# A recurrence step reordered: query times key, its masking and the next right sides

## The reference

```
attn  = where(causal, q_i @ k_i.T, 0)
u_adj = u_i - w_i @ S                      # u = T vc, w = T kbc, T the inverse of a triangular matrix
o_i   = q_i @ S + attn @ u_adj
S     = S + k_i.T @ u_adj
```

## Time and profile before

| | us |
|---|---|
| median of 3 runs (2459.3 to 2461.65) | 2460.59 |
| profiled execution, its own time | 2465.9 |
| its span | 2463.3 |
| TensorE busy | 2157.7 (88%) |
| VectorE busy | 1235.2 (50%) |
| ScalarE busy | 905.7 (37%) |
| GpSimd busy | 576.3 (23%) |

### The profile page before, as it was taken

One profiled execution on the slowest core, in us unless ns is written; L12 is line 12 of the kernel. 1 busy time (PEld: TensorE's weight loads), 2 busy tenths in 40 slices (PEclk: granted clock), 3 DMA queues, 4 the chain that ended last, 5 costly groups with the idle time before them and its releaser, 6 DMA issues.

```text
span 2463.3 us, 40437 instructions
## 1 busy us (share of the span) xinstructions
PE 2157.7 (88%) x15412; PEld 1857.6 (75%) x15412; DVE 1235.2 (50%) x1846; ACT 905.7 (37%) x1420; POOL 576.3 (23%) x416
## 2 busy tenths in 40 slices
PE   7887865655799999944999999999999999999998
PEld 5776755555688888833888888888888888888887
DVE  5776757896556776755143323432343233323332
ACT  4454530002233333324344434443444344434442
POOL 2555555896343444310000000000000000000000
PEclk9999977887799999976999999999999999999999
DMA  3558768787877887733000000000000000000000
GB/s 128 189 197 204 198 194 202 195 210 243 223 179 177 197 206 191 170 119 124 1 18 17 0 17 17 17 0 17 17 17 0 17 17 17 0 17 17 18 1 18
DMA packets 342570, 234.45 MB, mean 95 GB/s; under 512 B 280946, under 2 KB 315250, under 8 KB 331890
## 3 DMA queue, kind: packets, MB, share of 16 engines
q1 hardware_dynamic: 334258, 232.65, 34.2%
q10 hardware_dynamic: 8256, 1.05, 0.4%
HBM read 145.31 MB, written 88.34 MB: 95 GB/s over the span
## 4 chain that ended last, share of the span: by engine, by line
PE 51%; issue 1%; DVE 1%; ACT 0%; DMA 0%; POOL 0%; DVEq 0%; SPq 0%; ACTq 0%; POOLq 0%
PE B L1611 46%; PE O L1639 5%; PE T L1569 1%; DVE yb L1738 0%; ACT gate L1677 0%; DMA x<-x_s 0%; DVE stats L1769 0%; ACT L1677 0%; DVE z L1764 0%; DVE xl L1718 0%; DVE z L1760 0%; DVE z L1783 0%; ACT xh L1665 0%; POOL rstd L1819 0%; DVEq L1733 0%
## 5 line engine op out<-in xcount | busy, mean ns | idle before, releaser
L1611 PE MATMUL B<-act1l,wr 128*128 128x512 f32 x1024 | 398.5, 389 | 0.0
L1611 PE MATMUL B<-act0h,wr 128*128 128x512 f32 x1024 | 398.3, 389 | 0.0
L1611 PE MATMUL B<-act0l,wr 128*128 128x512 f32 x1024 | 398.3, 389 | 0.0
L1611 PE MATMUL B<-act1h,wr 128*128 128x512 f32 x1024 | 398.3, 389 | 0.0
L1691 ACT ACTIVATE yb<-B,scol 128x512 f32<-128x512 f32 x256 | 176.2, 688 | 581.1 <-PE B L1611 581.1
L1726 DVE TENSOR_TENSOR act0l<-yb,act0h 128x512 fp32r<-128x512 f32 x256 | 176.1, 688 | 378.0 <-ACT act0h L1694 375.8
L1816 POOL TENSOR_TENSOR rstd<-mv,ln_eps 128x4 f32<-128x4 f32 x16 | 3.2, 199 | 1305.0 <-DVE mv L1777 1305.0
L378 DVE SCALAR_TENSOR_TENSOR acc<-proj,taps,acc 128x512 f32<-128x512 f32 x288 | 214.4, 750 | 95.2 <-ACT acc L333 86.6
L1726 DVE TENSOR_TENSOR act1l<-yb,act1h 128x512 fp32r<-128x512 f32 x128 | 88.6, 692 | 295.5 <-ACT act1h L1694 295.5
L223 PE MATMUL proj<-xt,w_qkv 128*128 128x262 f32 x768 | 195.7, 402 | 37.7 <-DMA xt<-in_xt 20.9
L1611 PEld LDWEIGHTS B<-act1h,wr 128*128 128x128 f32 x1024 | 192.3, 188 | 39.9
(11 more groups left out here) (163 smaller groups left out, 3468.6 us busy)
## 6 DMA issues: line engine op xcount, KB each, us to landing
qk_s<-yT SPq DMA_DIRECT2D x16, 1024.0 KB, 5.8
kk_s<-kfull SPq DMA_DIRECT2D x16, 1024.0 KB, 3.9
qk<-qk_s SPq DMA_DIRECT2D x16, 1024.0 KB, 5.4
lt<-kk_s SPq DMA_DIRECT2D x15, 1024.0 KB, 5.3
wraw<-in_ffn_w SPq DMA_DIRECT2D x11, 1024.0 KB, 7.3
toe<-in_firp SPq DMA_DIRECT2D x64, 160.0 KB, 3.3
xt<-in_xt SPq DMA_DIRECT2D x16, 524.0 KB, 3.9
k_s<-ktok SPq DMA_DIRECT2D x16, 512.0 KB, 3.8
```

The source lines that it names most:

```text
L1611: last = nc.tensor.matmul(B[slot % 4][:, :], w, part, start=(k == 0 and i == 0), stop=(k == kts - 1 and i == len(parts) - 1))
```

## The change

In the ring's list, Q moves from behind W to behind T (for a step with both: N, T, Q, W, A, B, C). TensorE issues Q right behind T, ahead of the waits of the solve. VectorE evacuates Q as the first thing of its step, and computes the right side of step t+1 behind C's eviction of step t, ahead of the head norm and the layer norm; the right side of step 0 stands ahead of the first step. The streams of ScalarE, GpSimd and SyncE are as they were. No instruction is added or left out.

```diff
--- before.py
+++ after.py
@@ -843,7 +843,7 @@
         def rounds(pre, tail):
             n, q, a, b, c = ([(kind, g, "act" if kind in "NAB" else "dve") for g in range(4)] for kind in "NQABC")
             t, w = ([(kind, g, "act" if kind == "T" else "dve") for g in range(2)] for kind in "TW")
-            return (n if pre else []) + (t if tail else []) + (w if tail else []) + (q + a + b + c if pre else [])
+            return (n if pre else []) + (t if tail else []) + (q if pre else []) + (w if tail else []) + (a + b + c if pre else [])
 
         PRE, FULL, LAST = rounds(True, False), rounds(True, True), rounds(False, True)
 
@@ -1084,13 +1084,14 @@
                     from_state(t, p)
                     run("N", *rest)
                     run("T", *rest)
+                    run("Q", *rest)
 
                     pe.wait_ge(edges_done, t + 1)
                     pe.wait_ge(dve_out, last_c)
                     solve(t, p)
                     run("W", *rest)
                     outputs(t, p, n)
-                    run("QABC", *rest)
+                    run("ABC", *rest)
 
                 run("NQABC", PRE, 0, 0, 0, 0, 0, 0)
                 d, a = used(PRE, "dve"), used(PRE, "act")
@@ -1291,12 +1292,11 @@
                     last.then_inc(x1_done, 1)
 
                 def step(t, p, ntail, seq, round0, dve0, act0, pre, tail):
-                    right_side(t, p)
+                    if pre:
+                        evacuate("Q", seq, round0, t + 1, 1 - p)
                     if tail:
                         residual(t - 1, 1 - p, ntail, seq, round0)
                     outputs(t, p)
-                    if pre:
-                        evacuate("Q", seq, round0, t + 1, 1 - p)
                     head_sums(t)
                     if tail:
                         spread(t - 1, 1 - p, dve0 + used(seq, "dve", 1 + next(i for i, x in enumerate(seq) if x[:2] == ("W", 1))))
@@ -1308,6 +1308,7 @@
                         add_term("B", seq, act0, t + 1, 1 - p)
                     if pre:
                         evacuate("C", seq, round0, t + 1, 1 - p)
+                        right_side(t + 1, 1 - p)
                     head_norm(t)
                     if tail:
                         layer_norm(t - 1, 1 - p)
@@ -1331,6 +1332,7 @@
                         dve.wait_ge(act_out, 4)
                         dve.wait_ge(second_in, 16)
                         nc.vector.tensor_copy(lt[:, :, :], att[1][:, :, :]).then_inc(lt_moved, 1)
+                right_side(0, 0)
                 step(0, 0, 0, PRE, NPRE, used(PRE, "dve"), used(PRE, "act"), True, False)
                 with dve.Fori(0, MID // 2) as i:
                     for j in range(2):
```

## The result

The changed kernel takes 2469.43 us (median of 11 runs, 2464.47 to 2472.51) against 2460.59 before (11 runs, 2457.89 to 2462.53): a ratio of 1.0035, 95% interval 1.0027 to 1.0044, 6.6 to 10.8 us more. It is slower, as forecast, and inside the range; the forecast of 1.0024 lies just under the interval. The profiled execution of the changed kernel took 2466.87 us (span 2464.7), only 1.0 above that of before, so the profiles are compared stage by stage and not by their spans: the first N of the recurrence starts at 623.96 us after and at 627.09 before, and the feed-forward part behind the stage is 2.0 us shorter after, in code that the change does not touch.

What follows compares the result with a forecast made beforehand. TensorE was taken to bound the recurrence, with one 1.50 us hole per step. Fourteen intervals +4.8, step 0 +2.0 and the last step -1.0 made +5.8 us: 2466.4 us, ratio 1.0024, range 2460 to 2474.

Steps and rivals of the forecast that it cites:

- Step 1: On TensorE, query times key moved behind T costs its full 2.00 us per step, with no new waits.
- Step 2: Behind the state update, A starts at once; ScalarE's squares, ending at 3.87, delay its copies; TensorE alone starts N at 9.64.
- the rival in which the C eviction does not hold N: N starts at 9.64, 0.41 earlier than forecast; +0.1 us in all, 2460.7, no change; chance 0.28.
- Step 3: VectorE between mixture sum and C eviction gains 1.30 us, not 2.48; N waits for that eviction, starts at 10.05.
- Step 4: Right sides go ahead of head norm and layer norm, ready long before the solve; saves 0.24 us per step, 3.3 in all.
- the second stall: In some steps a long layer norm delays the right sides and the solve waits; forecast to go, 3.3 us in all.
- The sum: Whole kernel: period 27.30 us, fourteen intervals +4.8, first step +2.0, last step -1.0, together +5.8 us.
- the rival of the late loads: N waits for a last diagonal block landing 1.5 us later; +14 us on top, about 2480; chance 0.08.
- step 15: Last step of the recurrence, without query times key; solve forecast to start at 14.0 instead of 14.99, -1.0 us.
- step 0: First step of the recurrence, ahead of its first state update; query times key there forecast to add +2.0 us.

Runs made afterwards that it cites:

- experiment 3: Changed kernel with VectorE's layer-norm statistics put ahead of the head sums: 2458.06 us, ratio 0.9998 to the kernel before.
- experiment 4: Changed kernel with ScalarE's squares put behind the four A copies: 2485.14 us, ratio 1.0101 to the kernel before.
- experiment 9: Kernel before with one edit, VectorE's masks ahead of the sum with the mixture: 2511.39 us, ratio 1.0195.
- Experiment 2: Kernel before with one edit, the next step's right sides behind C, ahead of the head norm: 2459.63 us, ratio 0.9996.
- experiment 5: Changed kernel with squares behind A copies, statistics and add A ahead of head sums: 2459.0 us; second kernel, statistics also ahead of outputs: 2457.64 us.
- experiment 6: Second kernel of experiment 5 with key products and diagonal blocks loaded some 7 us earlier: 2473.66 us, ratio 1.0053 to the kernel before.
- experiment 8: Kernel before, query times key unmoved, masks ahead of the mixture sum, other reorderings: 2444.47 us with blocks loaded early, 2441.0 us with loads as before.

## Why the prediction was right

By its own steps:

- *Step 1, query times key counts in full:* right. It takes 2.0 us between T and the solve in every step, its data, its banks and W wait for nothing.
- *Step 2, ScalarE's squares are late next:* right. They end at 3.87, B waits 1.43 (about 1.3 named), products from the state start at 7.60 against 7.75. The copies were over-counted by 0.37 us. By their measured length TensorE alone would start N at about 9.4, as experiment 3 shows, and not at 9.64, so the rival in which the C eviction does not hold N should have said some 3 us faster and not no change. In experiment 3 the same slip shows as 0.2 us per step.
- *Step 3, VectorE gains 1.30 and not 2.48, and N waits for the C eviction:* right to 0.1 us (9.65 forecast and measured for C; N 9.98 against 10.05, so it gains 1.49 and not 1.42; N itself takes 3.81 us where it took 3.71, which takes that back). Experiment 3 shows that this wait sets the period, experiments 4 and 9 that lengthening the same chain costs step by step even where it removes TensorE's largest hole.
- *Step 4, the second stall goes:* right. No wait ahead of the solve, although the layer norm still takes up to 3.02 us. Experiment 2 gives it alone 2.5 us in these intervals, 3.3 were forecast.
- *The sum:* 14 intervals 382.36 us (662.26 to 1044.62) against 377.39, +4.97 where +4.8 was forecast. Twelve of the 14 are 27.32. One was 27.88: its last block was issued at 722.91, landed 3.7 us later, and N started at 726.74, 0.56 late, although the C eviction stood at its usual 9.65. That is the rival of the late loads, with 0.5 us in all. The first is 26.62: step 0 has no step before it whose statistics VectorE would take, so the C eviction starts at 8.20 and N at 9.38. The forecast had neither, and that the two nearly cancel is luck.
- *The term that was mis-sized is step 15:* forecast -1.0, measured +0.5 (from state update to state update 26.23 us against 25.73). The head norm ended where I had put it, so T started at 12.91. But TensorE had been idle for 3.36 us by then, 1.38 before, and came back slowly:

```profile
1057.53 1.78 PE L1022 MATMUL R<-const,o 128*128 128x128 f32 x8 [3.36 <-DVE o L1260]
1059.24 2.95 PE L1050 MATMUL Y<-x,tt 128*64 128x64 f32 x64
```

```profile
1043.00:1057.50 14.50, 9.74 (x170) 9.24 (x166) 12.23 (x25) 3.86 (x9) 5.02 (x4) 1.00 0.00 0
1057.50:1060.00 2.50, 2.47 (x22) 2.15 (x24) 1.27 (x4) 1.19 (x2) 0.00 (x0) 0.55 0.15 64
1060.00:1062.20 2.20, 2.20 (x57) 2.13 (x53) 0.00 (x0) 0.60 (x1) 0.00 (x0) 0.73 0.98 268
```

The granted clock behind that wait is 0.55, then 0.73; before, T took 1.09 and the solve 2.09 at 1.00. T and solve cost 1.5 us more than at the higher level. That clock is what the forecast left out: it had the solve at 14.0, and it started at 14.62. The Trainium skill, TensorE: Matmul & The Clock Gate, section HAM oscillation — how this bites in real kernels, says that idle gaps between bursts of matmuls bring the clock down; the traces agree, here and in experiments 2, 4, 5, 6 and 9, but not behind every gap: waits of the same length were followed by either level.

With step 0 (+2.0 forecast; 1.1 between the profiles, where the second N waited for its loads for 2.97 us against 4.31) the profiles account for some 6.6 us, or 7.5 with the 2.0. Against these the sum of +5.8 had 1.5 us too little in step 15 and 0.9 too much in step 0. The mechanism is what the experiments show; that the sum came this near is in part luck. The ratio says 8.6, with 6.6 as its lower end. What may be left, 1 to 2 us, I could not place; two single executions cannot settle it, since the untouched stages differ by more.

The Trainium skill, SBUF — State Buffer, section Who interferes with whom, says that a VectorE operation with two SBUF inputs contends with a GpSimd one that reads SBUF; I had set that rule against the trace. It did not hold add A up here either: add A runs 887.03 to 888.84 under a power on GpSimd of 886.18 to 889.09, at its old 1.81 us. That does not refute the rule. The other way round the trace agrees with it: in the kernel of experiment 3 GpSimd's small addition starts under add A and takes 1.73 us, where it takes 0.22 in the changed kernel, beside the statistics.

```profile
827.17 1.81 DVE L1207 TENSOR_TENSOR tt<-tdiag,r 96x768 f32<-96x768 f32 x2
827.33 1.73 POOL L1375 TENSOR_TENSOR ss<-ss,head_eps 128x16 f32<-128x16 f32 x1 [10.61 <-DVE ss L1253]
```

## What to carry to other kernels

A hole on the bounding engine names only its last releaser. Before work is moved into that engine's full stretch, add up what is late next in the stretch that it leaves, on every engine in its program order: here 3.56 us were freed, 1.5 could be used, and 2.1 were paid. With the squares, the sums, the statistics, the masks and the loads reordered as well, the kernel was 1% faster than before; most of that came without the move too (experiment 8), whose own share is at most some 0.3 us per step. And a queue behind an operation that another engine can hold must be empty of anything that the bounding engine waits for.

## What the runs showed of the hardware

- Four VectorE operations of the layer norm take 1.37 us alone, 2.95 when they meet one GpSimd product, 4.57 under two (experiment 9) and 6.75 when three run through them (experiment 6): 1.6, 3.2 and 5.4 us more, each time somewhat less than the products' own length. That each of the operations meets a product of its own is my reading and was not tried by itself.
- A small GpSimd operation is held by VectorE: the addition of 128x16 took 1.73 us when it started under add A (experiment 3) and 0.22 clear of it. Add A was not longer under GpSimd's power of 2.91 us.
- A hole of TensorE can cost more than its length, by the clock, and its length alone does not say whether. N took 5.44 us instead of 3.8 behind waits of 2.17, 2.27 and 2.51 us, and 3.81 behind waits of 2.27, 2.51 and 2.83 of the same kernel (experiment 4); in experiment 5 a wait of 1.79 us was once followed by an N of 5.43 us. What tells the two kinds of steps apart is open.
